# Cross attention: the order around the spreading of reciprocals, and their copy on ScalarE

## The reference

```python
Q = (q @ W_q.T + b_q).reshape(b, -1, NH, HD).transpose(0, 2, 1, 3)
K = (k @ W_k.T + b_k).reshape(b, -1, NH, HD).transpose(0, 2, 1, 3)
V = (v @ W_v.T + b_v).reshape(b, -1, NH, HD).transpose(0, 2, 1, 3)
scores = jnp.einsum('bhqd,bhkd->bhqk', Q, K) / math.sqrt(HD)
scores = jnp.where(causal, -jnp.inf, scores)
scores = jnp.where(padding_mask[:, None, None, :], -jnp.inf, scores)
attn = jax.nn.softmax(scores, axis=-1)
out = jnp.einsum('bhqk,bhkd->bhqd', attn, V)
return out.transpose(0, 2, 1, 3).reshape(b, -1, H) @ W_o.T + b_o
```

## Time and profile before

| what | value |
| --- | --- |
| median of three runs | 4476.57 us (4475.96 to 4482.53) |
| the profiled execution | 4481.21 us, span 4479.5 us |
| mean granted clock of TensorE, 1 is 2.4 GHz | 0.961 |
| busy, share of the span | TensorE 91%, VectorE 70%, ScalarE 37%, GpSimd 23% |
| reciprocals (line 1879) | 32, 0.24 us each |
| spread (line 1992) | 1024 narrow matmul records in 32 spreads |
| copy of the spread (line 1889) | 32, 0.68 us each |
| product (line 1891) | 32, 0.69 us each |
| first and last spread | from 2357.4 to 3500.0 us after the span's start |

### The profile page before, as it was taken

The page is one execution under the profiler, slowest core; times in us unless marked ns, Lnnn a source line. Parts: engine busy times, 40 slices in busy tenths (PEclk is TensorE's granted clock), DMA queues, the critical chain, the costliest instruction groups (busy, mean ns, idle before and its releaser), DMA issues. The chain is left out here.

```text
span 4479.5 us, 71612 instructions
## 1 busy us (share of the span) xinstructions
PE 4064.1 (91%) x26200; PEld 3023.7 (68%) x26200; DVE 3152.3 (70%) x6457; ACT 1652.2 (37%) x3472; POOL 1034.0 (23%) x597
## 2 busy tenths in 40 slices
PE   6999999998799999999778888898898799999999
PEld 5767676765566666666466676576576478787877
DVE  5787878774489999899657647657557566666664
ACT  3434343432333333343237537447357311111111
POOL 0333434343055555555500000000000000000000
PEclk8999999999899999999889999999999899999999
DMA  2110111001201111111143142242341310101000
GB/s 107 37 37 29 38 42 39 28 35 39 86 26 51 44 39 45 51 44 37 40 175 100 62 142 84 92 134 62 117 126 50 121 34 24 34 22 36 27 26 19
DMA packets 150049, 266.40 MB, mean 59 GB/s; under 512 B 30276, under 2 KB 36424, under 8 KB 149704
## 3 DMA queue, kind: packets, MB, share of 16 engines
q1 hardware_dynamic: 149704, 261.83, 17.5%
HBM read 164.88 MB, written 88.34 MB: 57 GB/s over the span
## 5 line engine op out<-in xcount | busy, mean ns | idle before, releaser
L1866 DVE TENSOR_REDUCE xa_mn<-xa_s 128x1 f32<-128x896 f32 (+7 forms) x512 | 373.0, 751 | 135.8 <-PE xa_s L1961 134.8
L1781 ACT ACTIVATE xa_src<-xa_s,xa_mn 128x896 f32<-128x896 f32 (+7 forms) x512 | 377.7, 740 | 231.6 <-DVE xa_mn L1866 230.3
L1967 PE MATMUL xa_gen<-xa_ident,xa_src 128*128 128x128 f32 x2304 | 310.2, 278 | 53.3 <-ACT xa_pT L1790 26.3
L73 PE MATMUL ff_wb<-ff_w_hi,ff_st_hi 128*128 128x512 f32 x768 | 323.8, 422 | 10.4 <-DVE ff_parts L2472 10.4
L940 DVE SCALAR_TENSOR_TENSOR mb_cv<-mb_xc,mb_cw,mb_cv 128x256 f32<-128x256 f32 x432 | 310.8, 773 | 31.9 <-ACT mb_xc L746 27.8
L1728 POOL TENSOR_TENSOR xa_res<-xa_res,xa_bor 128x512 f32<-128x512 f32 x32 | 40.5, 1270 | 1244.7 <-DMA xa_res<-after_mamba_dram 1244.7
L74 PE MATMUL ff_wb<-ff_w_hi,ff_st_lo 128*128 128x512 f32 x768 | 311.9, 406 | 0.0
L75 PE MATMUL ff_wb<-ff_w_lo,ff_st_hi 128*128 128x512 f32 x768 | 311.1, 405 | 0.0
L1967 PEld LDWEIGHTS xa_gen<-xa_ident,xa_src 128*128 128x128 f32 x2304 | 251.1, 143 | 75.1 <-ACT xa_src L1781 59.5
L1309 PE MATMUL mb_ib<-mb_wc,mb_yT 128*128 128x512 f32 x512 | 262.6, 661 | 1.8 <-DVE mb_y L1078 1.0
L2240 POOL TENSOR_TENSOR ff_mixed<-ff_at,ff_rw 128x1024 f32<-128x1024 f32 x32 | 60.9, 1904 | 875.3 <-DVE ff_at L2500 875.3
(11 more groups left out here) (494 smaller groups left out, 11031.7 us busy)
## 6 DMA issues: line engine op xcount, KB each, us to landing
xa_qa<-xa_q_dram SPq DMA_DIRECT2D x384, 64.0 KB, 2.0
xa_q_dram<-xa_kq SPq DMA_DIRECT2D x32, 512.0 KB, 2.8
xa_k_dram<-xa_kq SPq DMA_DIRECT2D x32, 512.0 KB, 2.8
xa_ka<-xa_k_dram SPq DMA_DIRECT2D x192, 64.0 KB, 2.0
xa_st<-xa_k_dram SPq DMA_DIRECT2D x192, 64.0 KB, 2.0
mf_xg<-in_x_dram SPq DMA_DIRECT2D x16, 512.0 KB, 5.1
turned_dram<-mf_xt_hi SPq DMA_DIRECT2D x16, 512.0 KB, 2.7
turned_dram<-mf_xt_lo SPq DMA_DIRECT2D x16, 512.0 KB, 4.0
```

Source lines behind the costliest of these rows:

```text
L73: nc.tensor.matmul(out, w_hi, x_hi, start=first, stop=False)
L1781: a_.activation(pq[:, hh, 0:w], s1[g, i, hh][:, 0:w], ACT.Exp, scale=-1.0, bias=mn[:, i % 2, hh:hh + 1], accum_out=sums[:, i // QT, i % QT ...
L1866: v_.tensor_reduce(mn[:, i % 2, hh:hh + 1], s1[g, i, hh][:, 0:(i + 1) * P], AX.X, ALU.min).then_inc(mx_ready.sem, 1)
L1967: last = tr(ps[:, n * P:(n + 1) * P], pq[:, hh, j * P:(j + 1) * P], ident[:])
```

## The change

`spread` moves from behind the product `av` to behind the next tile's first score. The copy of the spread bank is a step of its own, `copy`, and goes from VectorE to ScalarE, behind the new tile's first exp. VectorE's product (`scale`) moves from behind the first score (and its minimum) to behind the second. The spread's bank is released by ScalarE's copy (`sp_ready`) and no longer by the product (`head_ready`). The waits of the copy go with it. At the end of a batch the three steps stand behind the loop.

```diff
                 yield from one("score", 0)
                 if scale:
-                    yield "scale", scale.pop()
+                    yield "spread", scale[0]
                 yield from turns(0)
                 yield from one("exp", 0)
+                if scale:
+                    yield "copy", scale[0]
                 yield from one("score", 1)
+                if scale:
+                    yield "scale", scale.pop()
                 yield from turns(1)
...
                 if last:
                     yield "av", last
                 if done:
-                    yield "spread", (last[0], last[1] // QT)
                     scale.append((last[0], last[1] // QT))
...
+            yield "spread", scale[0]
+            yield "copy", scale[0]
             yield "scale", scale.pop()
...
             if what == "spread":
-                gen += [(("spread", *n), head_ready, NQB * n[0] + n[1])]
+                gen += [(("spread", *n), sp_ready, NQB * n[0] + n[1])]
...
+                def copied(g, b):
+                    act.wait_ge(bc_full.sem, bc_full.at(it, NQB * g + b))
+                    act.wait_ge(o_moved[b].sem, o_moved[b].at(it, g - 1))
+                    if g == 0:
+                        act.wait_ge(stored[b].sem, stored[b].at(it, -1))
+                    if g == 1:
+                        act.wait_ge(kq_stored[0].sem, kq_stored[0].at(it, 2 * NHG - 1))
+                    a_.activation(os[g][:, b, :], gen["spread", g, b][:], ACT.Copy).then_inc(sp_ready.sem, 1)
...
                 def scaled(g, b):
-                    dve.wait_ge(bc_full.sem, bc_full.at(it, NQB * g + b))
                     dve.wait_ge(av_full.sem, av_full.at(it, g * NT + QT * (b + 1) - 1))
-                    dve.wait_ge(o_moved[b].sem, o_moved[b].at(it, g - 1))
-                    if g == 0:
-                        dve.wait_ge(stored[b].sem, stored[b].at(it, -1))
-                    if g == 1:
-                        dve.wait_ge(kq_stored[0].sem, kq_stored[0].at(it, 2 * NHG - 1))
-                    v_.tensor_copy(os[g][:, b, :], gen["spread", g, b][:]).then_inc(sp_ready.sem, 1)
                     dve.wait_ge(sp_ready.sem, sp_ready.at(it, NQB * g + b))
                     v_.tensor_tensor(os[g][:, b, :], acc["o", g, b][:], os[g][:, b, :], ALU.mult).then_inc(head_ready.sem, 1)
```

More of the change, by code:

```diff
@@ L1735, in _ @@
         def _(act):
-            for s in [shi_ready, kqhi_ready, p_ready, pta_ready]:
+            for s in [shi_ready, kqhi_ready, p_ready, pta_ready, sp_ready]:
                 s.start(act)
@@ L1790, in turned @@
                     a_.activation(pT[:, k, 0:w], gen["turn", g, i, k][:, 0:w], ACT.Copy).then_inc(pta_ready.sem, 1)
-                return {"split": split, "src": source, "kq": channels, "exp": exps, "turn": turned}
+                def copied(g, b):
[6 more added lines that the diff above has]
+                    a_.activation(os[g][:, b, :], gen["spread", g, b][:], ACT.Copy).then_inc(sp_ready.sem, 1)
+                return {"split": split, "src": source, "kq": channels, "exp": exps, "turn": turned, "copy": copied}
             run(batch)
@@ L1798, in _ @@
             for s in [mask_ready, xn_ready, slo_ready, kqlo_ready, v_ready, mx_ready, ptv_ready, rs_ready,
-                      head_ready, sp_ready, out_ready, dve_step]:
+                      head_ready, out_ready, dve_step]:
                 s.start(dve)
```

## The result

The changed kernel takes 4492.86 us (median of ten runs, 4486.09 to 4496.98), the kernel before 4477.32 in the runs beside them. The ratio is 1.0032, with a 95% interval of 1.0023 to 1.0040: **slower by 14 us** (10 to 18). The forecast was +17.5 us. The profiled execution has a span of 4492.8 (4479.5 before).

A forecast was written before the change was run, and what follows sets the result against it. No engine is full; round trips between engines bound the stage. +3.7 us at A, +8.6 at B and +5.2 for clock falls sum to +17.5, from the median 4476.57 to 4494.1 us; range 4477 to 4506.

The forecast's parts named there:

- A: 16 places, spread behind tile 3's product, next tile 5: third pack 0.23 us later each, +3.7 us (-0.5 to 5.1).
- B: 12 places, spread behind tile 7's product, a group following: tile 0's product 0.72 us later each, +8.6 us (5.5 to 9.7).
- The clock: Stretches from spread to spread at a lower granted clock: 5 more falls at 1.05 us, +5.2 us (0 to 19).
- a slope by idle time: More TensorE idle time, more falls: 0.43 us more at B makes 3 falls, 0.23 at A makes 2.
- C: 4 places, the last spread of a batch, nothing to follow: 0.1 us shorter or longer on VectorE, no effect on the time.
- The wait for the bank goes: Rival: the third pack's and tile 4's 23.7 us wait for the spread's bank goes, 4452.9 us; ten in a hundred.
- the point that I had named: Whether ScalarE's copy at A ends before 2361.39; behind exp 0, only if exp 0 started by 2359.89.
- The next tile absorbs B: Rival: VectorE's idle 0.83 us before tile 2's first minimum catches up B's 0.72, 4481.4 us; eighteen in a hundred.
- The clock falls at nearly every place: Rival: falls at nearly all places add 19 us, 31.3 us slower in all, 4507.9 us; seven in a hundred.

The follow-up runs named there:

- The kernel filled at B alone: Changed kernel plus 14 unused identity transposes on TensorE in the idle time ahead of tile 0's product at B: 4485.58 us, ratio 1.0017.
- The kernel changed at B alone: Against the kernel before, the change made only at each group's second block (B and C), A as before: 4492.10 us, ratio 1.0031.
- Filled at both: Changed kernel plus 14 unused identity transposes at B and 10 at A ahead of the third pack: 4478.37 us, ratio 0.9999.
- the spread in its old place: Changed kernel with the spread back behind the product and ScalarE's copy ahead of turn 0 and exp 0: 4437.98 us, ratio 0.9912.

## Why the prediction was right

- **A, +3.7 predicted, +2.1 measured.** Every start came within 0.1: the turns at 2358.87, predicted and measured; exp 0 at 2360.06 for 2360.12; the copy's end at 2361.53 for 2361.62 (all on the old time axis). Two terms were off. Exp 0 follows the start of pack 0's copy by 0.50 where it was 0.55: before, its minimum had ended as late as 2360.07, and the earlier score did give that back. And the copy starts 0.87 behind exp 0, not 0.90.
- **B, +8.6 predicted, +9.4 measured.** The chain was as said. The product starts 0.10 behind the end of the copy, and I had taken no time for that.
- **The clock, +5.2 predicted, +4.5 by this profile.** The sum came out; the working did not. I had 3 more falls at B and 2 more at A; there are 5 more at B and 2 fewer at A. That the sum agrees is luck. The kernel filled at B alone shows why a slope by idle time can't give it: falls left out at B turned up at A. The kernel changed at B alone shows it too: with A's idle time at 1.59 as before, 12 stretches from A had a fall and not 5. Filled at both, the falls were gone and the price was shown. Which of the places has one when both are idle is not settled.
- **C, nothing.** From C to the next batch's first A it is 129.0 to 130.5 us from product to product, 127.8 to 130.8 before; a copy's length either way can't be told there.
- **The rivals.** "The wait for the bank goes" was the true worth of a ScalarE copy, at the point that I had named: ahead of exp 0 instead of behind it. It came to more than the 23.7 us of the wait, since B gains too and the falls go. "The next tile absorbs B" fell: the 0.79 is passed on whole (18.95 for 18.15 to the next tile 3). "The clock falls at nearly every place" fell for this kernel, with 13 of 28.

The advice of the Trainium skill (TensorEngine Tiling (Array Packing), section PSUM Bottleneck) to empty the accumulators with ScalarE and VectorE both holds here where the copy stands in ScalarE's idle time (ratio 0.9920), and costs time where it stands behind an exp (1.0032). How much of the gain is the engine's and how much the earlier place's is open: an equally early copy on VectorE, with the same release, was not run.

## What to carry to other kernels

Before a step is moved to an idle engine, look at what stands ahead of it in that engine's own order: the same copy on the same engine was worth 36 us of gain or 14 of loss by one line of the order. An instruction that starts earlier is worth nothing if what reads its result stands behind something else; follow the reader, not the writer. Where an accumulator bank goes round, ask which instruction releases it, and let the earliest one do so.

## What was not expected of the hardware

Which stretches have a fall of the granted clock changes with small shifts in TensorE's idle time. With the third pack's idle time at A gone and that at B down to 1.06 (the spread in its old place), none of 28 stretches had a fall to 1.2 GHz, against 10 before; with 0.33 more idle time at B than in the changed kernel (2.62 for 2.29) there were 20. The length alone does not decide: with the same 1.59 at A, 5 of 16 stretches had one before and 12 in the kernel changed at B alone; with the same 2.29 at B, 10 of 12 in the changed kernel and 4 in that one. Transposes of no use in both idle times gave 15 us back. In these kernels the falls are worth from 11 us of gain to 26 of loss, as much as the moves themselves.
